# Joining an expert's two sorted slot lists by a reversed identity product instead of a second sort

## The chip, the cores and the metric

The kernel runs on one core of one Trainium2 chip. The metric is the device time of the whole program in microseconds (us), as a median of several runs. All engines of the core work at once, each through its own queue of instructions: TensorE (PE), VectorE (DVE), ScalarE (ACT), GpSimd (POOL) and SyncE (SP, which here only issues DMAs). They are held to one another by semaphores alone.

## What is computed

Two transformer layers, each a gated cross-attention and a gated feed-forward, over 2048 tokens of 256 numbers. The change lies in the feed-forward of the first layer, a mixture of 64 experts: each token chooses 8 experts, and each expert takes its tokens in token order up to a capacity of 128; what comes later is dropped.

```python
E, K = 64, 8
CAP = 128
def _moe_experts(x, topk_idx, topk_w, w_gate, w_up, w_down):
    flat_e = topk_idx.reshape(-1)
    rows = jnp.repeat(jnp.arange(n), K)
    oh = jax.nn.one_hot(flat_e, E, dtype=jnp.int32)
    pos = jnp.cumsum(oh, axis=0) - oh
    pos = jnp.take_along_axis(pos, flat_e[:, None], axis=1)[:, 0]
    valid = (pos < CAP).astype(x.dtype)
    p = jnp.minimum(pos, CAP - 1)
    buf = jnp.zeros((E, CAP, H), x.dtype).at[flat_e, p].add(x[rows] * valid[:, None])
    g = jnp.einsum('ech,ehi->eci', buf, w_gate)
    u = jnp.einsum('ech,ehi->eci', buf, w_up)
    y = jnp.einsum('eci,eih->ech', jax.nn.silu(g) * u, w_down)
    y_tok = y[flat_e, p] * (topk_w.reshape(-1) * valid)[:, None]
    return jnp.zeros((n, H), x.dtype).at[rows].add(y_tok)
```

The result is a sum over the slots of an expert, row by row; the order of the tokens within the 128 slots doesn't enter it, only which tokens are in.

## The kernel before

The program goes through four stages, one after the other: the attention of layer one (to about 400 us), its routing and experts (400 to 744 us), the attention of layer two, and its mixture of 8 experts. The tokens are worked in 4 groups of 512.

**Routing.** For each group of tokens the kernel computes scores and the 8 chosen experts of each token. To each pair of token and chosen expert it gives a key, larger the earlier the token comes, and zero where the expert isn't chosen. `keyT` holds the keys transposed: partition e is expert e with the tokens of the first half (0 to 1023), partition 64 + e is the same expert with the tokens of the second half, 1024 keys to a partition.

**Slot lists.** Inside the DVE program, `largest(dst, src)` finds the 128 largest keys of each partition in order, 8 at a time: 16 times a `max` (L901; the trace calls it MAX8), and between them 15 times a `match_replace` (L904), which strikes out the 8 just found. The trace shows each `match_replace` as two instructions, MATCH_VALUE_LOAD and MATCH_REPLACE8. Each instruction waits for the one before. `largest` runs twice: over `keyT` into `cand` (all 128 partitions, 1024 keys each), which leaves two sorted lists to an expert, one on partition e and one on 64 + e; then, after a DMA by SP has laid the second list beside the first (L407, `cand[0:64, 128:256]`), over these 256 candidates into `slots` (64 partitions). PE transposes `slots` (L1742), ACT copies the result out of PSUM into `slotsT` (L1370), slot by partition and expert by column. The rest of this part waits for it:

```python
dve.wait_ge(t_ring.free, T3)
sl.add(dve.tensor_scalar(part[0][:, 0:E0], slotsT[:], -1.0, float(K0 * T), ALU.mult, ALU.add))
sl.add(dve.tensor_scalar(part[1][:, 0:E0], slotsT[:], 0.0, None, ALU.is_equal))
...
sl.add(dve.tensor_tensor(dst_idx[:], src_idx[:], part[1][:, 0:E0], ALU.add))
```

`src_idx` is the row of the DRAM tensor `table` to gather for each slot (an empty slot has key 0 and takes the row of zeros, 2048). `dst_idx` is the row to add to; an empty slot gets 2048 + its own partition, so that the 128 rows of an expert are always different ones.

**Experts.** 32 steps of two experts. For each step POOL issues two indirect gathers of 128 rows (L479, `xg` from `table`), PE transposes the rows (L1750), multiplies (L1764, L1777), DVE scales into `y` (L947), and POOL issues two indirect DMAs that add the rows to two DRAM sums, `acc` (L489); each waits until the one before it on the same sum has landed. Gathers run three steps ahead. SP loads the weights of 8 experts ahead and then one step's for each step done.

**Rings.** PE writes PSUM banks in turn within a ring, here `t_ring` with two banks. Each fill has a fixed position; `full` counts fills, `free` counts reads. PE waits before a fill until the position two back has been read; a reader waits for its own position. T3 is the position of the first fill of the experts.

Of the kernel before, what the change touches and what calls it, by code (L numbers as in the profile page):

```python
# [8 lines left out]
ACT = mybir.ActivationFunctionType  # L9
ALU = mybir.AluOpType  # L10
AX = mybir.AxisListType

P = 128
# [5 lines left out]
NG = NT // G  # L19
C = DIM // P  # L20
H0, D0 = 16, 128
E0, I0, K0 = 64, 88, 8
CAP = 128
# [78 lines left out]
def flamingo(nc, a, out, stages=4):  # L102
    with ExitStack() as ctx:
        def sb(name, shape, dt=F32, scope=ctx):
            return scope.enter_context(nc.sbuf_tensor(name, shape, dt))

        def sem(name):
            return ctx.enter_context(nc.semaphore(name))
# [5 lines left out]
        t_ring = Ring([bank[4], bank[5]], sem("t_full"), sem("t_free"))  # L114
# [5 lines left out]
        ident = sb("ident", [P, P])  # L120
        ones = sb("ones", [P, P])
# [23 lines left out]
        before = sb("before", [P, 8, 8])  # L145
        key_base = sb("key_base", [P, NT])
        zeros = sb("zeros", [P, ROW])
        cand = sb("cand", [P, 2 * CAP])
        slots = sb("slots", [E0, CAP])
        slotsT = sb("slotsT", [P, E0])  # L150
        spare = sb("spare", [P, E0])
        src_idx = sb("src_idx", [P, E0], I32)
# [45 lines left out]
        keyT = sb("keyT", [P, T // 2], scope=rows)  # L198
# [102 lines left out]
        rows_ready = sem("rows_ready")  # L301
        slot_chain = sem("slot_chain")
        slots_ready = sem("slots_ready")
        cand_ready = sem("cand_ready")
        cand_moved = sem("cand_moved")
        idx_ready = sem("idx_ready")
        idx_now = sem("idx_now")
        w_loaded = [sem(f"w_loaded{q}") for q in range(4)]
# [32 lines left out]

        Q2, S2, T2 = Q_STEP * NG, S_PREP + S_STEP * NG, T_STEP * NG
        QR, SR, TR, TRF = 2, 2, 4, 3
        Q3, S3, T3 = Q2 + QR * NG, S2 + SR * NG, T2 + TR * NG + 1
        NQ = E0 // 8
        Q4, S4, T4 = Q3 + 4 * NQ, S3 + 4 * NQ, T3 + 4 * NQ
        QA, SA, TA = 4, 8, 18
# [8 lines left out]
        def _(sp):  # L356
# [46 lines left out]
                    SKV - MAIN)).then_inc(w3_loaded, 16)  # L403
            sp.dma_start(ctx_rows[:], ctx_d[0:P, :]).then_inc(ctx_loaded, 16)

            sp.wait_ge(cand_ready, 1)
            sp.dma_start(cand[0:E0, CAP:2 * CAP], cand[E0:P, 0:CAP]).then_inc(cand_moved, 16)  # L407
            with sp.Fori(1, NQ) as i:
                for q in range(4):

# [39 lines left out]
        def _(pool):  # L450
            pool.memset(ident[:], 0.0).then_inc(ident_zero, 1)
            pool.wait_ge(ident_zero, 1)
            pool.memset(zeros[:], 0.0).then_inc(zero_ready, 1)
            pool.memset(before[:], 1.0).then_inc(ident_zero, 1)
            pool.iota(key_base[:], pattern=[[-K0 * P * G, NG], [K0 - K0 * P, G]], base=K0 * T + 1,
                      channel_multiplier=-K0, allow_small_or_imprecise_dtypes=True).then_inc(r_const, 1)
# [4 lines left out]
                               base=0, pattern=[[1, 8], [-1, 8]], channel_multiplier=0).then_inc(r_const, 1)  # L461
            pool.affine_select(out=ident[:], in_=ident[:], compare_op=ALU.not_equal, fill=1.0,
                               base=0, pattern=[[-1, P]], channel_multiplier=1).then_inc(const_ready, 1)

            def split_squares(i):
                for h in range(H0):
                    pool.wait_ge(q2_ready, H0 * i + h + 1)
                    pool.tensor_tensor(q2_lo[:, h % 3, :], q2[h % 2], q2_hi[:, h % 3, :],  # L468
                                       ALU.subtract).then_inc(q2_split, 1)
# [53 lines left out]
            for n in range(NA):  # L523
# [4 lines left out]
                               pattern=[[-D1, 8]], channel_multiplier=1).then_inc(mask_step, 1)  # L528
            pool.wait_ge(mask_step, 2)
            pool.affine_select(out=head_mask[:], in_=head_mask[:], compare_op=ALU.is_ge, fill=0.0, base=D1 - 1,  # L530
                               pattern=[[D1, 8]], channel_multiplier=-1).then_inc(mask_step, 1)
# [8 lines left out]
        def _(dve):  # L540
# [357 lines left out]
            def largest(dst, src):  # L898

                for r in range(CAP // 8):  # L900
                    sl.add(dve.max(dst[:, 8 * r:8 * r + 8], src))  # L901
                    sl.wait()
                    if r < CAP // 8 - 1:
                        sl.add(dve.match_replace(src, dst[:, 8 * r:8 * r + 8], src, 0.0))  # L904
                        sl.wait()

            largest(cand[:, 0:CAP], keyT[:])
            dve.drain().then_inc(cand_ready, 1)
            dve.wait_ge(cand_moved, 16)
            largest(slots[:], cand[0:E0, :])  # L910
            dve.drain().then_inc(slots_ready, 1)

            dve.wait_ge(t_ring.free, T3)
            sl.add(dve.tensor_scalar(part[0][:, 0:E0], slotsT[:], -1.0, float(K0 * T), ALU.mult, ALU.add))
# [310 lines left out]
        def _(act):  # L1225
            sr, tr, qr = s_ring.end(), t_ring.end(), q_ring.end()
# [129 lines left out]
            def route(i, half, last):  # L1356
                tr.at(T2 + TRF, TR, i)
                if not last:
                    route_front(i + 1)
                rows = slice(half * E0, (half + 1) * E0)  # L1360
                act.activation(keyT[rows, bass.ds(G * P * (i - half * (NG // 2)), G * P)], tr.read(act)[rows, :],
                               ACT.Copy).then_inc(t_ring.free, 1)
# [3 lines left out]
            with act.Fori(NG // 2, NG - 1) as i:  # L1366
                route(i, 1, False)
            route(NG - 1, 1, True)
            tr.at(T2 + TR * NG)
            act.activation(slotsT[:], tr.read(act)[:, 0:E0], ACT.Copy).then_inc(t_ring.free, 1)  # L1370

            def transposed(q):
                act.activation(xgT[:, q % 2], tr.read(act)[:].rearrange(
# [171 lines left out]
        def _(pe):  # L1545
            qr, sr, tr = q_ring.end(), s_ring.end(), t_ring.end()
# [192 lines left out]
            route(NG - 1, True)  # L1739
            tr.at(T2 + TR * NG)  # L1740
            pe.wait_ge(slots_ready, 1)
            pe.transpose(tr.fill(pe)[:, 0:E0], slots[:], ident[0:E0, 0:E0]).then_inc(t_ring.full, 1)  # L1742

            def transpose_rows(i, q):
                pe.wait_ge(xg_loaded[q], 32 * (i + 1))
# [295 lines left out]
```

## Time and profile before

| | us |
|---|---|
| median of 3 runs | 1337.47 |
| lowest and highest | 1336.98, 1337.78 |
| the profiled execution's own time | 1336.93 |
| its span, first to last instruction | 1335.2 |
| of it, the first search over `keyT` | 469.75 to 509.73 |
| from there to the first use of `slotsT` | 509.73 to 527.29 |
| experts, first PE work to the last scatter landed | 534.13 to 744.20 |

The profile is of one execution; its time lies 0.54 us under the median. Its page has the span in 40 slices of some 33 us with the busy tenths of each engine, the chain of work that ended last, and groups of instructions by line. From its trace come timelines (start, duration, engine, line, what), groups by shape, the chain in order of time, and busy times by stretch. PEclk is TensorE's granted clock: 0.50 is 1.2 GHz and 1.00 is 2.4 GHz, a number between is a mean over a stretch.

### The profile page before, as it was taken

What the parts mean: (1) busy time and instruction counts of PE and PEld (TensorE: products, weight loads), DVE (VectorE), ACT (ScalarE), POOL (GpSimd) and SP (SyncE); (2) the same over time, 40 slices, a digit from 0 to 9 for tenths busy, and PEclk for the clock granted to TensorE, in tenths of its full rate; (3) what the DMA queues carried; (4) which work ended last, traced back from release to release, by engine and by line L of the source; (5) the groups of instructions that cost most, each with busy time, mean ns of one, the idle gap of its engine ahead of it and who ended that gap; (6) DMA issues with size and microseconds to landing.
All of it is one profiled execution on the core that took longest, in us unless ns stands there. A gap on an engine that the chain in (4) does not pass through costs nothing.

```text
span 1335.2 us, 16322 instructions
## 1 busy us (share of the span) xinstructions
PE 1038.4 (78%) x5301; PEld 855.8 (64%) x5301; DVE 697.9 (52%) x1659; ACT 431.5 (32%) x793; POOL 278.2 (21%) x223
## 2 busy tenths in 40 slices
PE   5989979989766400776667368887989999999997
PEld 3867858778545300665556226564657989898996
DVE  6277586675758897222223477575675324232221
ACT  4565465554623100111111032324252232322221
POOL 0414214133000001788787110010100000000000
PEclk8999999999887655888787566757666999899899
DMA  7004000000001040788786540000000000000001
GB/s 266 3 0 137 1 1 1 0 1 1 1 0 40 24 126 11 170 173 180 166 186 120 144 164 1 2 0 0 0 0 0 1 1 0 0 0 0 0 0 64
DMA packets 58967, 66.36 MB, mean 50 GB/s; under 512 B 5037, under 2 KB 55719, under 8 KB 58151
## 3 DMA queue, kind: packets, MB, share of 16 engines
q1 hardware_dynamic: 45268, 46.48, 11.1%
q0 software_dynamic: 12288, 18.88, 8.1%
q8 instruction: 28, 0.46, 0.1%
q10 hardware_dynamic: 1363, 0.37, 0.1%
q14 instruction: 20, 0.16, 0.0%
HBM read 48.13 MB, written 17.56 MB: 49 GB/s over the span
## 4 chain that ended last, share of the span: by engine, by line
PE 54%; DVE 14%; issue 12%; DMA 6%; ACT 6%; POOL 6%; ACTq 0%; DVEq 0%; POOLq 0%; SPq 0%
PE bank L1959 12%; PE bank L1978 7%; DMA acc<-y,dst_now 5%; PE bank L1619 4%; PE bank L1664 4%; PE bank L1887 3%; PE bank L1845 3%; PE bank L1649 3%; POOL acc L489 2%; PE bank L1970 2%; POOL xg L479 2%; PE bank L1904 2%; POOL q_lo L468 2%; DVE cand L901 1%; PE bank L1804 1%
## 5 line engine op out<-in xcount | busy, mean ns | idle before, releaser
L1959 PE MATMUL bank<-gu_hi,xnT_split 128*128 128x352 f32 x640 | 158.7, 328 | 0.0
L468 POOL TENSOR_TENSOR q_lo<-soft,q_hi 128x512 fp32r<-128x512 f32 x64 | 93.2, 1456 | 236.8 <-ACT soft L1313 236.7
L1959 PEld LDWEIGHTS bank<-gu_hi,xnT_split 128*128 128x128 f32 x640 | 112.6, 190 | 1.0 <-issue 0.7
L479 POOL DMA_INDIRECT xg<-table,src_now x64 | 63.9, 999 | 216.5 <-DVE src_now L927 197.4
L489 POOL DMA_INDIRECT acc<-y,dst_now x64 | 102.3, 1599 | 26.7 <-issue 20.3
L1959 PE MATMUL bank<-gu_lo,xnT_split 128*128 128x352 f32 x320 | 103.8, 324 | 0.0
L1183 DVE SCALAR_TENSOR_TENSOR soft<-sg,combine_w,bank 128x176 f32<-128x176 f32 x160 | 56.4, 395 | 87.4 <-PE bank L1959 81.3
L1978 PE MATMUL bank<-dn,attnT 128*128 128x256 f32 x448 | 101.2, 384 | 0.0
L1978 PEld LDWEIGHTS bank<-dn,attnT 128*128 128x128 f32 x448 | 85.6, 194 | 11.2
L707 DVE COPY qT<-bank 128x512 f32<-128x512 f32 x64 | 44.2, 691 | 87.7 <-PE bank L1664 86.6
L1517 ACT ACTIVATE sg<-bank 128x352 f32<-128x352 f32 x80 | 37.1, 464 | 152.0 <-PE bank L1959 151.9
L947 DVE TENSOR_SCALAR y<-bank,xg 128x256 f32<-128x256 f32 x64 | 28.0, 480 | 106.6 <-PE bank L1777 106.6
L627 DVE SCALAR_TENSOR_TENSOR x<-bank,gates,x 128x256 f32 (+1 forms) x48 | 22.7, 482 | 114.0 <-PE bank L1978 94.8
L1764 PEld LDWEIGHTS bank<-xgT,w_gu 128*88 128x88 f32 x512 | 75.8, 193 | 6.7 <-issue 3.8
L1764 PE MATMUL bank<-xgT,w_gu 128*88 128x128 f32 x512 | 77.3, 316 | 0.7 <-issue 0.7
L1750 PE MATMUL bank<-ident,xg 128*128 128x128 f32 x128 | 25.7, 335 | 65.5 <-DMA xg<-table,src_now 65.5
L1309 ACT ACTIVATE q_hi<-qT 128x512 fp32r<-128x512 f32 x64 | 40.4, 630 | 91.3 <-DVE qT L707 91.2
L1619 PE MATMUL bank<-vw,attnT 128*128 128x256 f32 x256 | 62.1, 399 | 4.3 <-ACT attnT L1263 4.3
L1649 PE MATMUL bank<-kT,qT 128*128 128x64 f32 x512 | 64.0, 268 | 0.0
L1649 PEld LDWEIGHTS bank<-kT,qT 128*128 128x128 f32 x512 | 62.5, 191 | 1.4
L1750 PEld LDWEIGHTS bank<-ident,xg 128*128 128x128 f32 x128 | 17.4, 169 | 70.1 <-DMA xg<-table,src_now 56.5
L1959 PEld LDWEIGHTS bank<-gu_lo,xnT_split 128*128 128x128 f32 x320 | 60.7, 190 | 0.3
(256 smaller groups left out, 2140.1 us busy)
## 6 DMA issues: line engine op xcount, KB each, us to landing
w_gu<-in_L_ffn_w_gu SPq DMA_DIRECT2D x32, 352.0 KB
w_dn<-in_L_ffn_w_down SPq DMA_DIRECT2D x32, 176.0 KB
acc<-zeros SPq DMA_DIRECT2D x2, 2176.0 KB, 11.4
acc_rows<-acc SPq DMA_DIRECT2D x8, 512.0 KB, 4.9
gu<-in_L_gu SPq DMA_DIRECT2D x1, 3520.0 KB, 13.7
table<-xw SPq DMA_DIRECT2D x4, 640.0 KB
wo<-in_L_xattn_Wo SPq DMA_DIRECT2D x2, 1024.0 KB, 16.2
wq<-in_L_xattn_Wq SPq DMA_DIRECT2D x1, 2048.0 KB, 18.5
```

The lines of the kernel that those rows point to most:

```text
L468: pool.tensor_tensor(q2_lo[:, h % 3, :], q2[h % 2], q2_hi[:, h % 3, :], ALU.subtract).then_inc(q2_split, 1)
L479: pool.indirect_dma_start(xg[:, q, e, :], None, table, bass.IndirectOffsetOnAxis(ap=src_now[:, q, e:e + 1], axis=0)).then_inc(xg_loaded[q] ...
L489: pool.indirect_dma_start(acc[e], bass.IndirectOffsetOnAxis(ap=dst_now[:, q, e:e + 1], axis=0), y[:, q, e, :], None, compute_op=ALU.add).t ...
L707: dve.tensor_copy(qT[:, h % 3, :], qr.read(dve)[:]).then_inc(q_ring.free, 1)
L1183: ins = dve.scalar_tensor_tensor(out=act_v[:, j % 2, at:at + F1], in0=sg[:, (j + p) % 2, e * F1:(e + 1) * F1], scalar=combine_w[:, j, 2 * ...
L1619: mm = pe.matmul(o_banks[0][:, 0:DIM], attnT[:, j % 2, p, :], vw[:, j // 2, p, :], start=(p == 0), stop=(p == 7))
L1649: mm = pe.matmul(s_bank[0][:, at:at + SKV], qT[:, h % 3, j * P:(j + 1) * P], kT[:, h, (j // 2) * SKV:(j // 2 + 1) * SKV], start=True, stop ...
L1664: mm = pe.matmul(b[:], w[:, c, h * D0:(h + 1) * D0], v[:, c, :], start=(n == 0), stop=(n == len(terms) - 1))
L1750: mm = pe.transpose(b[:, at:at + P], xg[:, q, e, c * P:(c + 1) * P], ident[:])
L1764: mm = pe.matmul(b[0:I0, e * P:(e + 1) * P], w_gu[:, q, e, c, o:o + I0], xgT[:, q % 2, e, c, :], start=(c == 0), stop=(c == C - 1))
L1959: mm = pe.matmul(b[:, 0:2 * F1], v[:, c, j * P:(j + 1) * P], w[:, c, p, o, :], start=(n == 0), stop=(n == len(terms) - 1))
L1978: mm = pe.matmul(o_banks[j % 2][:, 0:DIM], attn_flat[0:n, f, :], dn1[0:n, f, :], start=(f == 0), stop=(f == FC - 1))
```

## The change

The second `largest` and the DMA between the two are gone. `cand` has 128 columns now, `slots` is gone. In their place come four products on PE and five instructions on DVE. With a_e the count of expert e's first list:

- PE transposes `cand` whole: the columns 0 to 63 are the first lists, the columns 64 to 127 the second, slot by partition. DVE copies this into `lists`.
- DVE marks the used slots of the first lists (`taken`), PE multiplies by a matrix of ones, and so each partition has a_e for each column e.
- DVE forms `keep` = (a_e + own partition number < 128), and `late` = second list times `keep`: of the second list the first 128 - a_e entries.
- PE sums identity times first list and `reversal` times `late` in one PSUM bank. `reversal` has its ones where row + column is 127; so the second list lies from slot 127 downward and meets the first nowhere.
- DVE copies the sum into `slotsT`, which ACT did before.

`reversal` is built by POOL at the start of the program with a memset and an affine_select. The ring `t_ring` has three fills here, not one, so T3 is two higher. The slots of an expert hold the same tokens in another order: second-half tokens stand in falling order at the end, and empty slots in the middle.

```diff
-        cand = sb("cand", [P, 2 * CAP])
-        slots = sb("slots", [E0, CAP])
+        cand = sb("cand", [P, CAP])
+        lists = sb("lists", [P, 2 * E0])
+        taken = sb("taken", [P, E0])
+        keep = sb("keep", [P, E0])
+        late = sb("late", [P, E0])
+        reversal = sb("reversal", [P, P])
...
-        Q3, S3, T3 = Q2 + QR * NG, S2 + SR * NG, T2 + TR * NG + 1
+        Q3, S3, T3 = Q2 + QR * NG, S2 + SR * NG, T2 + TR * NG + 3
...
-            sp.wait_ge(cand_ready, 1)
-            sp.dma_start(cand[0:E0, CAP:2 * CAP], cand[E0:P, 0:CAP]).then_inc(cand_moved, 16)
...
+            pool.memset(reversal[:], 0.0).then_inc(reversal_ready, 1)
             pool.memset(before[:], 1.0).then_inc(ident_zero, 1)
...
+            pool.wait_ge(reversal_ready, 1)
+            pool.affine_select(out=reversal[:], in_=reversal[:], compare_op=ALU.not_equal, fill=1.0,
+                               base=1 - P, pattern=[[1, P]], channel_multiplier=1).then_inc(reversal_ready, 1)
...
-            largest(cand[:, 0:CAP], keyT[:])
-            dve.drain().then_inc(cand_ready, 1)
-            dve.wait_ge(cand_moved, 16)
-            largest(slots[:], cand[0:E0, :])
+            largest(cand[:], keyT[:])
             dve.drain().then_inc(slots_ready, 1)
+            lr = t_ring.end()
+            lr.at(T2 + TR * NG)
+            dve.tensor_copy(lists[:], lr.read(dve)[:, 0:2 * E0]).then_inc(t_ring.free, 1)
+            lr.evacuated(dve)
+            dve.tensor_scalar(taken[:], lists[:, 0:E0], 0.0, None, ALU.is_gt).then_inc(list_step, 1)
+            dve.tensor_scalar(keep[:], lr.read(dve)[:, 0:E0], spare[:, 0:1], float(CAP), ALU.add,
+                              ALU.is_lt).then_inc(t_ring.free, 1)
+            lr.evacuated(dve)
+            dve.tensor_tensor(late[:], lists[:, E0:2 * E0], keep[:], ALU.mult).then_inc(list_step, 1)
+            dve.tensor_copy(slotsT[:], lr.read(dve)[:, 0:E0]).then_inc(t_ring.free, 1)
...
-            tr.at(T2 + TR * NG)
-            act.activation(slotsT[:], tr.read(act)[:, 0:E0], ACT.Copy).then_inc(t_ring.free, 1)
...
-            pe.transpose(tr.fill(pe)[:, 0:E0], slots[:], ident[0:E0, 0:E0]).then_inc(t_ring.full, 1)
+            pe.transpose(tr.fill(pe)[:, 0:P], cand[:], ident[:]).then_inc(t_ring.full, 1)
+            pe.wait_ge(list_step, 1)
+            pe.matmul(tr.fill(pe)[:, 0:E0], ones[:], taken[:], start=True, stop=True).then_inc(t_ring.full, 1)
+            pe.wait_ge(list_step, 2)
+            pe.wait_ge(reversal_ready, 2)
+            b = tr.fill(pe)[:, 0:E0]
+            pe.matmul(b, ident[:], lists[:, 0:E0], start=True, stop=False)
+            pe.matmul(b, reversal[:], late[:], start=False, stop=True).then_inc(t_ring.full, 1)
```

On DVE, between the last `max` over `keyT` and the arithmetic on `slotsT`, the program of before reads as follows (its first rows; the pair L904, L901 stands 15 times in all):

```order
550 L901 MAX cand<-keyT 128x8
551 L904 MATCH_REPLACE keyT<-cand,keyT 128x1024
552 L901 MAX cand<-keyT 128x8
553 L901 MAX slots<-cand 64x8
554 L904 MATCH_REPLACE cand<-slots,cand 64x256
555 L901 MAX slots<-cand 64x8
```

And the changed one in the same place:

```order
551 L910 MATCH_REPLACE keyT<-cand,keyT 128x1024
552 L907 MAX cand<-keyT 128x8
553 L917 COPY lists<-bank 128x128
554 L919 TENSOR_SCALAR taken<-lists 128x64
555 L920 TENSOR_SCALAR keep<-bank,spare 128x64
556 L923 TENSOR_TENSOR late<-lists,keep 128x64
557 L924 COPY slotsT<-bank 128x64
558 L927 TENSOR_SCALAR soft<-slotsT 128x64
```

Of DVE's 31 instructions over 64 partitions none is left; five over 128 partitions stand there.

On PE, between the last transposes of the routing (of keys in `soft`) and the first of the experts (of `xg`), before:

```order
795 L1734 MATMUL bank<-ident,soft 128x128 x4
796 L1742 MATMUL bank<-ident,slots 128x64
797 L1750 MATMUL bank<-ident,xg 128x128 x4
```

and now:

```order
795 L1745 MATMUL bank<-ident,soft 128x128 x4
796 L1753 MATMUL bank<-ident,cand 128x128
797 L1755 MATMUL bank<-taken,ones 128x64
798 L1759 MATMUL bank<-lists,ident 128x64
799 L1760 MATMUL bank<-late,reversal 128x64
800 L1768 MATMUL bank<-ident,xg 128x128 x4
```

One transposition has become four products, the last two into one bank.

## Rows read from the trace of the kernel before

**Rows 1.** Page, section 2: busy tenths in 40 slices of 33 us, DVE, POOL, PEclk

```profile
DVE  6277586675758897222223477575675324232221
POOL 0414214133000001788787110010100000000000
PEclk8999999999887655888787566757666999899899
```

**Rows 2.** Busy time by stretch: window, length, busy us (instructions), clock, DMA share, GB/s

```profile
core 0: us, PE busy (x) PEld busy (x) DVE busy (x) ACT busy (x) POOL busy (x), PEclk, DMA share, GB/s
470.00:509.75 39.75, 0.00 (x0) 0.00 (x0) 38.68 (x46) 0.00 (x0) 0.00 (x0) 0.50 0.32 85
509.75:527.29 17.54, 0.37 (x1) 0.18 (x1) 13.89 (x46) 0.22 (x1) 0.00 (x0) 0.50 0.01 2
534.13:744.20 210.07, 137.85 (x769) 120.73 (x769) 52.69 (x168) 31.23 (x64) 162.73 (x125) 0.80 0.77 161
```

**Rows 3.** Chain that ended last, in order of time: start, us, what

```profile
508.49 1.24 DVE cand L901
...
509.81 1.78 DMA cand<-cand
...
511.61 0.43 DVE slots L901
512.04 0.02 issue
512.06 0.49 DVE cand L904 x2
...
526.11 0.43 DVE slots L901
526.54 0.03 issue
...
526.63 0.38 PE bank L1742
527.01 0.02 issue
527.04 0.23 ACT slotsT L1370
527.27 0.02 issue
527.29 0.20 DVE soft L914
```

**Rows 4.** Prices of nearby operations: engine, line, shape, count, busy us, mean ns, idle before

```profile
L1742 PE MATMUL bank<-ident,slots 64*128 64x64 f32 x1 | 0.4, 367 | 57.5 <-DVEq L911 57.5
L1046 DVE COPY c<-bank 128x256 f32<-128x256 f32 x16 | 6.8, 423 | 14.3 <-PE bank L1887 14.3
L726 DVE TENSOR_SCALAR qvar<-bank 128x64 f32<-128x64 f32 x4 | 0.9, 214 | 0.0
L918 DVE TENSOR_TENSOR soft<-soft,spare 128x64 f32<-128x64 f32 x1 | 0.2, 217 | 0.0
L914 DVE TENSOR_SCALAR soft<-slotsT 128x64 f32<-128x64 f32 x1 | 0.2, 196 | 0.8 <-ACT slotsT L1370 0.8
```

**Rows 5.** Timeline, first expert step: start, duration, engine, line, what, idle before

```profile
529.72 1.15 POOL L479 DMA_INDIRECT xg<-table,src_now  x1 [197.36 <-DVE src_now L927]
534.13 1.11 PE L1750 MATMUL bank<-ident,xg 128*128 128x128 f32 x4 [7.13 <-DMA xg<-table,src_now]
535.28 0.60 ACT L1373 ACTIVATE xgT<-bank 128x512 f32<-128x512 f32 x1 [8.02 <-PE bank L1750]
535.98 3.54 PE L1764 MATMUL bank<-xgT,w_gu 128*88 128x128 f32 x16 [0.73 <-issue]
539.63 0.42 DVE L939 TENSOR_TENSOR act_h<-act_g,bank 88x256 f32<-88x256 f32 x1 [10.78 <-PE bank L1764]
540.11 1.13 PE L1777 MATMUL bank<-w_dn,act_h 88*128 88x256 f32 x4
541.43 0.42 SPq L383 DMA_DIRECT2D w_gu<-in_L_ffn_w_gu  x1
```

**Rows 6.** Timeline, first scatters of two steps in mid-stage and one later; same columns

```profile
588.65 1.62 POOL L489 DMA_INDIRECT acc<-y,dst_now  x1 [0.30 <-issue]
...
595.08 1.62 POOL L489 DMA_INDIRECT acc<-y,dst_now  x1 [0.30 <-issue]
...
724.54 1.62 POOL L489 DMA_INDIRECT acc<-y,dst_now  x1 [0.30 <-issue]
```

**Rows 7.** The chain's shares from 527 to 744 us; then `acc`'s landings

```profile
by line: issue 30.6%; DMA acc<-y,dst_now 30.4%; POOL acc L489 13.4%; POOL xg L479 11.4%; DMA xg<-table,src_now 6.0%; PE bank L1777 2.1%; PE bank L1764 1.6%; PE bank L1750 1.5%; DVE y L947 0.9%; POOLq L487 0.3%; DVE act_h L939 0.2%; DVE src_
DMA to landing us min/median/max: 3.8/4.4/14.6
```

**Rows 8.** Timeline, first 7 us of the program

```profile
0.81 0.20 POOL L451 MEMSET ident<- 128x128 f32 x1 [0.29 <-POOLq L2012]
2.08 0.28 POOL L462 TENSOR_SCALAR_AFFINE_SELECT ident<-ident 128x128 f32<-128x128 f32 x1
6.72 0.29 PEld L1551 LDWEIGHTS bank<-ident,ctx_rows 128*128 128x128 f32 x2 [6.72 <-issue]
```

**Rows 9.** Timeline of ACT, attention of layer two: the table load in each loop body

```profile
793.24 1.28 ACT L1397 ACT_TABLE_LOAD   x1
856.16 1.28 ACT L1397 ACT_TABLE_LOAD   x1
917.73 1.28 ACT L1397 ACT_TABLE_LOAD   x1
```

More of the change, by code:

```diff
@@ L303, in flamingo @@
         slots_ready = sem("slots_ready")
-        cand_ready = sem("cand_ready")
-        cand_moved = sem("cand_moved")
+        reversal_ready = sem("reversal_ready")
+        list_step = sem("list_step")
         idx_ready = sem("idx_ready")
```

## The prediction, made before the changed kernel ran

> **What bounds the kernel now.** I read the slices of the page first, for the place of the change. In slices 15 and 16 (some 467 to 534 us) DVE stands at 9 and 7 tenths while POOL is at 0 and 1, and the granted clock is at 5, its low level [rows 1]. Busy time by stretch says it more sharply: from 470 to 509.75 us and again to 527.29 us DVE is the only engine at work, PE runs one product, DMA has a share of 0.01 in the second stretch [rows 2]. Nothing runs beside the search that could take its place on the path, and nothing that is under way could hold the next stage back.
>
> Then the chain of waits, for the edges [rows 3]. The last `max` over `keyT` ends at 509.73. From there the chain goes through the DMA that moves the second lists, through 16 `max` and 15 `match_replace` on `slots`, one transposition on PE and one copy on ACT, and comes to the first arithmetic on `slotsT` at 527.29. This stretch of 17.56 us is what the change rewrites, and all of it lies on the path.
>
> Last, what follows. The first gather is issued at 529.72, after an idle time of POOL of 197 us that DVE's indices ended, and PE's first expert work waits for that gather's landing [rows 5]. Then POOL and the landings of the scatters set the pace: POOL is busy for 163 of 210 us [rows 2], of the chain 30.4% is landing of `acc` and 25% POOL's own issue of gathers and scatters [rows 7], and one step takes 595.08 - 588.65 = 6.43 us [rows 6]; from 588.65 to 724.54 are 21 steps, 6.47 us each, so the rhythm is even. SP's first further weight load, at 541.43, is let go by the first step's output, not by the clock on the wall [rows 5]. So the whole stage can start earlier as a block, and with it all that is behind.
>
> **What goes.** The DMA with its hops: 511.61 - 509.73 = 1.88 us. The second search: 16 x 0.43 (`max`) + 15 x 0.49 (`match_replace` with its load) + 30 gaps of some 0.02 = 14.93 us, the 526.54 - 511.61 of the chain. Transposition and copy with their hops: 527.29 - 526.54 = 0.75 us. Together 17.56 us [rows 3].
>
> **What comes**, step by step, on the same path, since each step needs the one before. The granted clock is 0.50 in this stretch, 1.2 GHz, after 40 us in which PE did nothing [rows 2], and a handful of small products gives me no reason to price them at the other level.
>
> 1. DVE's last `max` to PE: 0.09 us, as 526.54 to 526.63 [rows 3].
> 2. Transposition with 128 columns. That with 64 took 0.37 [rows 4]. A further 64 columns: 16 products of 128 columns took 3.54 us in the first expert step, 0.22 each, so 0.11 for 64 [rows 5]. 0.48.
> 3. Hop of 0.03 and DVE's copy of 128 columns from PSUM. The rows have 0.214 for 64 columns and 0.423 for 256 [rows 4]; on the line between, 0.28 to 0.29. Together 0.32.
> 4. `taken`: 0.20 as L914, and a gap of 0.02 [rows 3, 4]: 0.22.
> 5. Hop from DVE to PE 0.05 (540.05 to 540.11 [rows 5]), the product with ones 0.37, hop back 0.03: 0.45.
> 6. `keep` from PSUM 0.21 and `late` 0.22 with a gap of 0.02 between: 0.45 [rows 4].
> 7. Hop 0.05, first product 0.37, the second behind it 0.11, hop 0.03: 0.56.
> 8. Copy into `slotsT` 0.21, gap 0.02: 0.23.
>
> The sum is 0.09 + 0.48 + 0.32 + 0.22 + 0.45 + 0.45 + 0.56 + 0.23 = 2.80 us. The gain is 17.56 - 2.80 = 14.76 us.
>
> Bounds. Two terms are not shown by any row as they will stand: a product right behind another of 64 columns with other weights, and the hops into a PE that waits for two semaphores. If the second product costs its full 0.37 and each of the three later hops 0.09 more (one more hop of the kind of step 1), the new chain takes 2.80 + 0.26 + 0.27 = 3.3, and with 0.3 more for what I overlook, 3.6. If the hops are all 0.02 and the copies no dearer than 0.21, it takes 2.5. So the gain lies between 13.9 and 15.1 us; I stay at 14.76, since the nearest rows are of just this kind of chain.
>
> The rows price a product by its columns: 0.22 us for 128 columns at the low clock [rows 5]. The Trainium skill ("FP8 and Floating Point Precision", TensorE Precision Notes) has true FP32 take four passes through the array, which would be 4 x 128 / 1.2 GHz = 0.43 us for 128 columns, as an estimate. The row holds about half of that. By the page's price the 64 further columns of step 2 and the second product of step 7 would cost 0.21 each, the new chain 3.0 us and the gain 14.6.
>
> **What is moved or added elsewhere.** POOL builds `reversal`: a memset ahead of the work on `ident`, 0.20 us, and an affine_select behind it, 0.28 [rows 8]. So `ident` is ready at 2.56, not 2.36, and PE first wants it at 6.72, when the data has landed: hidden, with 4.2 us to spare. If that cover were gone it would cost 0.2 us. ACT loses one copy; its next instruction waits for PE at 535.28 anyway [rows 5]. SP loses a wait and a DMA; behind them stood only weight loads that are held by the experts' first output. The ring gives no new wait: the third fill needs the first one read (step 3, long done), and the experts' first fill needs the second one read (step 6); the bank is the same one as before, since T3 rises by two.
>
> The arithmetic behind `slotsT`, the four index copies, the 0.85 us to POOL's first gather and the landing of that gather are untouched and move as they are. What is late next is this gather, as now; nothing else is near, as the first stretch's DMAs (share 0.32) have given way to 0.01 after 509.75 [rows 2].
>
> The sum against the profiled execution: 1336.93 - 14.76 = 1322.2. The median of the runs lies 0.54 above that execution, so I forecast 1322.7 us.
>
> **Rivals.**
>
> *A, the clock falls otherwise.* The attention of layer two runs at mean clocks of 0.5 to 0.7 [rows 1], so PE is there often at the low level, and a shift of all by 14.8 us could make other stretches slow or fast. The price is in the table loads, which mark the same place of one loop body: 856.16 - 793.24 = 62.92 and 917.73 - 856.16 = 61.57 us [rows 9]. Two passes over the same code differ by 1.35 us; over four groups that is at most 5.4 if all fall on one side, more likely 1 to 3. Time: 1317 to 1328. For it: the clock there is really unsettled. Against it: three runs of before lie within 0.80 us, so that what differs from run to run doesn't reach the total. The level follows from what PE did before, and that sequence stays the same once the block has moved. The Trainium skill ("TensorE: Matmul & The Clock Gate", What's actually happening) adds that the moment at which the clock is let up is not tied to the kernel's start and varies from run to run; by that rule a shift of the block is one more draw of what the three runs drew already, which speaks for small.
>
> *B, the order of rows makes the scatters slower, and the kernel ends slower than before.* The slots hold the same rows in another order: the second list falls, and empty slots, which all gather row 2048, stand in the middle. If the DMAs of an expert landed later for it, the steps would stretch, since 30.4% of 217 us, 66 us, are landings of `acc` on the chain [rows 7]. To eat up 14.8 us and 2.7 more for a result called slower, these 66 us must grow by 17.5, or 27%: a median landing of 5.6 instead of 4.4 us. At that point it decides; 10% (4.8 us) would give back 6.6 us and end at 1329. Against it: the number and size of rows are unchanged, rows of an expert are scattered over the table anyway, and 21 steps with experts of whatever load went by at an even 6.47 us [rows 6].
>
> *C, the change doesn't free the path.* Something other than the slots would hold the first gather: a table write, the zeroing of the sums, weights. Then it would end at 1337.5 minus little. The DMA share of 0.01 in the stretch and POOL's wait that DVE ended [rows 2, 5] speak against it.
>
> **How the numbers follow.** Forecast as summed (gain of 13.9 to 15.1 with a scatter of 1 us more either way): 0.82. A with more than 2 us in either direction: 0.11. B giving back a part: 0.03; B to a slower kernel: 0.02. C: 0.02. The range takes the bounds of the unknown terms (1322.4 to 1323.6), the typical 1 to 3 us of A on both sides, and nothing of B beyond that: 1319.5 to 1326.5 us. What lies outside is the rest of A (0.03), B and C. About 0.2%, 2.7 us, is what a measurement of this kernel can tell from no change. Faster by more than that: 0.82 + 0.11 + 0.03 = 0.96, of which I leave 0.01 for the edge of B: 0.95. Within it: C and that edge, 0.03. Slower: 0.02.
>
> **What would show it.** In the profile after: no DMA from `cand`, a stretch of 2.5 to 3.6 us from the last `max` to the first arithmetic on `slotsT`, at a granted clock of 0.50; the first gather near 515.0 instead of 529.72; steps of 6.43 to 6.47 us; the last scatter landed near 729.4 instead of 744.20; passes of 60 to 63 us in the attention of layer two. I am wrong if the new stretch is above 4 us (then a hop or a product is mis-sized), if the expert steps are longer (B), or if the two later stages together differ from 591.0 us (1335.2 - 744.2) by more than 3 (A).

## The result and the profile after

| | us |
|---|---|
| changed kernel, median of 4 runs (lowest, highest) | 1320.73 (1319.32, 1321.93) |
| kernel before, median of 4 runs beside it | 1337.22 (1334.33, 1337.78) |
| ratio, 95% interval | 0.9884 (0.9870 to 0.9899) |
| profiled execution of the changed kernel, its span | 1319.32, 1317.6 |

Faster by 16.5 us, with an interval of 13.5 to 17.4 us; the forecast was 1322.7 us in 1319.5 to 1326.5, a gain of 14.8. In two later series of runs the same kernel took 1321.60 us (6 runs, ratio 0.9895, 0.9874 to 0.9917) and 1320.77 us (5 runs, 0.9888, 0.9867 to 0.9909). Over all series the kernel before has 39 runs with a mean of 1336.60 us and the changed one 15 with 1321.51: a difference of 15.1 us.

The place of the change, in the timeline of the profiled execution: start, duration, engine, line, operation, and in brackets the idle time before it and what ended that. It answers to [rows 3].

```profile
508.18 1.23 DVE L907 MAX8 cand<-keyT 128x8 f32<-128x1024 f32 x1
509.52 0.47 PE L1753 MATMUL bank<-ident,cand 128*128 128x128 f32 x1 [40.75 <-DVEq L914]
510.03 0.29 DVE L917 COPY lists<-bank 128x128 f32<-128x128 f32 x1 [0.62 <-PE bank L1753]
510.36 0.20 DVE L919 TENSOR_SCALAR taken<-lists 128x64 f32<-128x64 f32 x1
510.61 0.69 PE L1755 MATMUL bank<-taken,ones 128*128 128x64 f32 x2 [0.61 <-DVE taken L919]
511.33 0.28 DVE L920 TENSOR_SCALAR keep<-bank,spare 128x64 f32<-128x64 f32 x1 [0.78 <-PE bank L1755]
511.65 0.22 DVE L923 TENSOR_TENSOR late<-lists,keep 128x64 f32<-128x64 f32 x1
511.93 0.69 PE L1759 MATMUL bank<-lists,ident 128*128 128x64 f32 x2 [0.63 <-DVE late L923]
512.41 0.64 PE L1760 MATMUL bank<-late,reversal 128*128 128x64 f32 x2
513.09 0.23 DVE L924 COPY slotsT<-bank 128x64 f32<-128x64 f32 x1 [1.21 <-PE bank L1760]
513.34 0.20 DVE L927 TENSOR_SCALAR soft<-slotsT 128x64 f32<-128x64 f32 x1
...
515.77 1.15 POOL L485 DMA_INDIRECT xg<-table,src_now  x1 [183.67 <-DVE src_now L940]
```

I call the stretch from the end of the last MAX8 (508.18 + 1.24 = 509.42) to the first use of `slotsT` (513.34) the join. It is 3.92 us, where it was 17.56: the join itself gave 13.64 us. The first gather follows 2.43 us behind, as it did behind 527.29 [rows 3, 5]. What to see on PE's lines is the count: the transposition is one instruction (x1), each of the three other products is two (x2).

The same by stretch: length, busy us and count of each engine, granted clock, DMA share, GB/s. The first two answer to the second and third line of [rows 2]; the last two are loop passes in the attention of layer two, each from one of ACT's table loads, shown below, to the next.

```profile
core 0: us, PE busy (x) PEld busy (x) DVE busy (x) ACT busy (x) POOL busy (x), PEclk, DMA share, GB/s
509.42:513.34 3.92, 2.28 (x7) 1.61 (x7) 1.22 (x5) 0.00 (x0) 0.00 (x0) 0.50 0.00 0
520.19:729.92 209.73, 138.89 (x769) 121.47 (x769) 53.59 (x168) 31.28 (x64) 162.88 (x125) 0.80 0.77 161
...
777.60:838.10 60.50, 50.85 (x187) 34.63 (x187) 42.34 (x97) 21.19 (x37) 4.05 (x4) 0.72 0.01 2
838.10:899.52 61.42, 50.65 (x187) 35.18 (x187) 38.33 (x90) 21.21 (x37) 4.05 (x4) 0.72 0.00 1
```

```profile
777.60 1.28 ACT L1408 ACT_TABLE_LOAD   x1
838.10 1.28 ACT L1408 ACT_TABLE_LOAD   x1
899.52 1.28 ACT L1408 ACT_TABLE_LOAD   x1
```

In the kernel before, the same two passes, from 793.24 and from 856.16 [rows 9], were

```profile
793.24:856.16 62.92, 52.94 (x187) 37.01 (x187) 40.97 (x94) 21.20 (x36) 4.04 (x4) 0.67 0.01 2
856.16:917.73 61.57, 52.81 (x187) 36.79 (x187) 38.36 (x90) 21.21 (x37) 4.04 (x4) 0.67 0.00 1
```

PE has the same 187 products in each, busy for 52.9 us at a clock of 0.67 and for 50.7 at 0.72. So of the 17.6 us between the two profiled spans, 13.64 are the join; 0.31 lie ahead of it (509.73 against 509.42, where only POOL's two instructions at the start of the program are new); 0.35 in the experts, from the first gather to POOL's first instruction after the last scatter (214.53 against 214.18); and 3.3 in the two later stages (590.95 against 587.65), which the change doesn't touch. Of these 3.3 us, 2.42 lie in the first of the two passes and 0.15 in the second; the part ahead of them is 1.34 us shorter (47.65 against 48.99), and what follows them is 0.61 us longer (418.08 against 417.47). In the second pass PE is busy for 2.2 us less and the pass is only 0.15 us shorter, so the mean clock alone doesn't set the length of a pass. The experiments ask what these 3.3 us are, why the join took 3.92 and not 2.80 us, and whether it can be shorter.

### The profile page after: what moved, and what is told of

The parts are those of the page before. It is cut to its first block and busy times, and to the rows that moved or that the text cites. A ratio compares the mean times of both kernels' runs of the same rounds, so it can differ in the third digit from the quotient of the medians.

```text
span 1317.6 us, 16309 instructions
## 1 busy us (share of the span) xinstructions
PE 1034.8 (79%) x5307; PEld 852.9 (65%) x5307; DVE 686.0 (52%) x1618; ACT 431.5 (33%) x792; POOL 278.8 (21%) x225
## 3 DMA queue, kind: packets, MB, share of 16 engines
HBM read 48.13 MB, written 17.56 MB: 50 GB/s over the span
## 5 line engine op out<-in xcount | busy, mean ns | idle before, releaser
L1782 PEld LDWEIGHTS bank<-xgT,w_gu 128*88 128x88 f32 x512 | 79.5, 202 | 7.6 <-issue 5.6
L1782 PE MATMUL bank<-xgT,w_gu 128*88 128x128 f32 x512 | 82.9, 331 | 0.7 <-issue 0.7
L1384 ACT ACTIVATE xgT<-bank 128x512 f32<-128x512 f32 x32 | 19.1, 597 | 152.5 <-PE bank L1768 152.5
```

The source lines that it names most:

```text
L1782: mm = pe.matmul(b[0:I0, e * P:(e + 1) * P], w_gu[:, q, e, c, o:o + I0], xgT[:, q % 2, e, c, :], start=(c == 0), stop=(c == C - 1))
```

## Experiments

The surplus is what the total gained beyond the join's 13.64 us. Three theories of it: the later stages draw anew from some sequences of clock levels in each run (1, scatter); the new place in time fixes another sequence (2, place); something in the kernel is faster for good (3).

**The changed kernel again**, without an edit, for more runs.

> The changed kernel once more, for the size of its gain with more runs. Its first profile had 13.6 us from the join itself, 0.3 from the stages ahead of it, 0.3 from the experts and 3.3 from the attention of layer two (17.6 in all). Theory 1 (the 3.3 us are scatter of the clock, a draw that falls anew in each run): the difference of medians comes down towards 13.6 to 14.5 us, and runs of one kernel differ by up to 3 us. Theory 2 (the new position in time sets another sequence of clock levels for good) and theory 3 (something else in the kernel, such as the order of rows or the addresses, is faster for good): the difference stays at 16 to 17 us.

1321.60 us (1319.30 to 1324.70, 6 runs), the kernel before 1336.42 (1333.37 to 1339.79, 15 runs), a difference of medians of 14.8 us, between what theory 1 (13.6 to 14.5) and the other two (16 to 17) had forecast. Join 3.93 us. Here the search ended at 510.76, 1.3 us later than in the first profile, and the two passes took 62.79 and 60.32 us. So one and the same program has other passes from one execution to the next (60.50 and 61.42 us in the first profile), and the runs of one kernel spread over 5.4 and 6.4 us. Both speak for theory 1, but the changed kernel's own median stayed within 1 us of the first.

**Pads behind the join**: 11, 6 and later 2 dependent passes of DVE over `keyT`, which nobody reads any more.

```diff
             dve.tensor_copy(slotsT[:], lr.read(dve)[:, 0:E0]).then_inc(t_ring.free, 1)
+            for _ in range(6):
+                sl.add(dve.tensor_scalar(keyT[:], keyT[:], 1.0, None, ALU.mult))
+                sl.wait()
```

> The changed kernel with 11 dependent passes of DVE over 128x1024 numbers behind the join, some 11 x 1.25 = 13.7 us, so that the experts start where they did before the change. Theory 1: the time of the changed kernel plus the length of the pad, some 1334.5 us, and within 1 us of the kernel before if that draws the same lot. Theory 2: exactly the time of the kernel before, and the clock levels of its attention of layer two (0.67 in the loop passes) come back. Theory 3: some 2 to 3 us under the kernel before, though all starts at the same moment.

> The same with 6 passes, some 7.5 us. Theories 1 and 3: the changed kernel plus 7.5 us within 1 us. Theory 2: off this line by 1 to 3 us in either direction, since a third position draws a third sequence of clock levels.

A pass took 0.72 us, not 1.25: DVE's line of the 11 passes and the one of the 6, in the two timelines,

```profile
514.93 7.97 DVE L927 TENSOR_SCALAR keyT<-keyT 128x1024 f32<-128x1024 f32 x11
```

```profile
514.39 4.33 DVE L927 TENSOR_SCALAR keyT<-keyT 128x1024 f32<-128x1024 f32 x6
```

So the pads were 7.9 and 4.3 us, and the first didn't put the block back where it was; it started its gathers 4.4 us earlier than the kernel before (525.36 against 529.72). My estimate had taken MATCH_REPLACE8's 1.21 us for 1024 columns as the price of any pass. The times are 1331.79 (10 runs) and 1327.67 us (6 runs), 10.6 and 6.5 us above 1321.2, the middle of the changed kernel's two medians so far, for pads of 7.9 and 4.3: both slower by 2.2 to 2.7 us than the pad. Taken by the expectation, with 4.3 in place of 7.5 us, the run with 6 passes misses theories 1 and 3 (within 1 us) and falls where theory 2 had put it (off by 1 to 3 us). Against theory 2 stands the profile with 6 passes. Its experts end 9.4 us earlier than those of the kernel before (734.81 against 744.25), and yet the two passes have the kernel before's length to 0.01 us, at its clock:

```profile
783.80:846.72 62.92, 52.94 (x187) 37.01 (x187) 40.96 (x94) 21.21 (x36) 4.04 (x4) 0.67 0.01 1
846.72:908.29 61.57, 52.81 (x187) 36.78 (x187) 38.37 (x90) 21.22 (x37) 4.04 (x4) 0.67 0.00 1
```

The same two passes, begun at another moment: a pass falls into a small set of lengths (over all profiles 60.3 to 60.5, 61.4 to 61.6 and 62.7 to 62.9 us), and being later or earlier doesn't by itself choose. That the clock makes the difference is argued, not shown: the passes of 60.3 to 60.5 us all have a mean clock of 0.72 and those of 62.7 to 62.9 us have 0.67 or 0.70, but those of 61.4 to 61.6 us occur at 0.67, 0.69, 0.70 and 0.72.

**The join by a maximum.** The first list is zero just in the slots where the second belongs, and each key of the second half is smaller than each of the first. So neither a count nor a mask is needed. ACT copies the transposed first list out, while DVE reverses the second.

```diff
-            dve.tensor_copy(lists[:], lr.read(dve)[:, 0:2 * E0]).then_inc(t_ring.free, 1)
...
-            dve.tensor_copy(slotsT[:], lr.read(dve)[:, 0:E0]).then_inc(t_ring.free, 1)
+            dve.tensor_copy(rev[E0:P, :], cand[E0:P, ::-1]).then_inc(list_step, 1)
+            lr.skip(1)
+            b = lr.read(dve)
+            dve.wait_ge(t_ring.free, T3 - 1)
+            dve.tensor_tensor(slotsT[:], b[:, 0:E0], lists[:, 0:E0], ALU.max).then_inc(t_ring.free, 1)
...
+            act.activation(lists[:, 0:E0], tr.read(act)[:, 0:E0], ACT.Copy).then_inc(t_ring.free, 1)
...
+            pe.transpose(tr.fill(pe)[:, 0:E0], cand[0:E0, :], ident[0:E0, 0:E0]).then_inc(t_ring.full, 1)
+            pe.wait_ge(list_step, 1)
+            pe.transpose(tr.fill(pe)[:, 0:E0], rev[E0:P, :], ident[E0:P, E0:P]).then_inc(t_ring.full, 1)
```

> The join in another way: keys of the first half are all larger than keys of the second, and the first list is zero where the second belongs, so slotsT is the maximum of the first list and the second one read backwards. DVE copies the second lists backwards while PE transposes the first and ACT copies them out; PE transposes the second, DVE takes the maximum. No product with ones, none with reversal. From the last max over keyT to the first arithmetic on slotsT: copy 0.3, hop 0.05, transposition 0.45, maximum 0.25, hops 0.1, some 1.2 us against 3.92. All theories: 2.7 us under the changed kernel, some 1318 us; if only the full fp32 products are dear, as the trace of the changed kernel says, the four transpositions and copies cost no more than that.

The join is as expected (1.09 against some 1.2 us). Timeline, same columns:

```profile
510.84 1.23 DVE L908 MAX8 cand<-keyT 128x8 f32<-128x1024 f32 x1
512.18 0.36 PE L1754 MATMUL bank<-ident,cand 64*128 64x64 f32 x1 [40.75 <-DVEq L915]
512.21 0.22 DVE L918 COPY rev<-cand 64x128 f32<-64x128 f32 x1
512.49 0.36 PE L1756 MATMUL bank<-ident,rev 64*128 64x64 f32 x1
512.58 0.22 ACT L1382 ACTIVATE lists<-bank 128x64 f32<-128x64 f32 x1 [40.52 <-PE bank L1754]
512.91 0.22 DVE L922 TENSOR_TENSOR slotsT<-bank,lists 128x64 f32<-128x64 f32 x1 [0.48 <-PE bank L1756]
513.17 0.20 DVE L925 TENSOR_SCALAR soft<-slotsT 128x64 f32<-128x64 f32 x1
```

From 512.08 to 513.17 it is 1.09 us, 2.83 less than in the changed kernel. Each PE line is x1, each some 0.36 us. The time was 1321.41 us (6 runs), only 0.2 us under the changed kernel in the same series and 3.4 above the 1318 that I had expected. In this profile the search ends at 512.08, 1.3 us later than in the changed kernel's second profile, and the experts take 215.24 instead of 212.74 us. Since neither stage was edited, I ran it again.

> The join by the maximum once more, since its join took 1.09 us as expected (2.83 under the changed kernel) but its median of 6 runs lay only 0.2 us under it. If that was scatter (its profiled execution had the search end 2.7 us later than that of the changed kernel, ahead of the join): 1318 to 1320 us, 16.5 to 18 us under the kernel before in the same call. If something in this form costs the 2.6 us back for good: 1321 to 1322 us, and the same stage longer again in the profile.

1318.29 us (1317.71 to 1321.74, 5 runs), 17.45 us under the kernel before beside it (ratio 0.9870, 0.9849 to 0.9891); join again 1.09 us. The two medians of the same program disagree by 3.1 us, more than the 2.8 us in question. The mean of the 11 runs is 1320.61 us, against 1321.51 for the 15 of the changed kernel: the total doesn't settle which is faster. That the join itself is shorter by 2.83 us is shown in both profiles.

**The counting product in fp32r**, one execution. fp32r is a 32-bit type for operands of PE; the counted numbers are 0 and 1, which it holds exactly.

```diff
-        taken = sb("taken", [P, E0])
+        taken = sb("taken", [P, E0], F32R)
+        ones_r = sb("ones_r", [P, P], F32R)
...
+            dve.tensor_copy(ones_r[:], ones[:]).then_inc(list_step, 1)
             largest(cand[:], keyT[:])
...
-            pe.matmul(tr.fill(pe)[:, 0:E0], ones[:], taken[:], start=True, stop=True).then_inc(t_ring.full, 1)
+            pe.matmul(tr.fill(pe)[:, 0:E0], ones_r[:], taken[:], start=True, stop=True).then_inc(t_ring.full, 1)
```

> The changed kernel with the ones and the marks taken rounded to fp32r for the counting product (both hold only 0 and 1, so the sums stay exact). In the changed kernel this product shows as two pairs of weight load and MATMUL, 0.69 us for 64 columns. If a full fp32 product is dear because it goes through the array as two instructions: one pair here, some 0.35 us, and the join 3.92 - 0.34 = 3.6 us. If it is dear for another reason (the wait, the weights of ones): 0.69 us as before.

Timeline:

```profile
513.55 0.42 PE L1757 MATMUL bank<-taken,ones_r 128*128 128x64 f32 x1 [0.61 <-DVE taken L921]
...
514.61 0.69 PE L1761 MATMUL bank<-lists,ident 128*128 128x64 f32 x2 [0.64 <-DVE late L925]
```

One instruction and 0.42 us, where the full fp32 product beside it still has two and 0.69. The join is 3.66 us, 0.26 shorter. So what is dear is the second instruction of a full fp32 product, not the wait ahead of it, which is the same (0.61 us idle in both kernels). The whole run took 1326.05 us, 4.5 above the changed kernel's mean. Its search ended at 512.36, ahead of the join and up to 2.9 us later than in other profiles, and the two later stages took 592.17 us. What follows the two passes took 422.10 us here, 422.03 in the second profile of the kernel before and 420.64 in the run with PE kept busy, against 417.35 to 418.50 in the ten other profiles. Since the unedited kernel before does it too, I take this for scatter and not for the edit; why it differs is open.

**PE kept busy ahead of the join**, one execution (1326.68 us).

```diff
+            pe.wait_ge(o_read, 2 + 2 * NT)
+            pe.wait_ge(slot_chain, 26)
+            for n in range(10):
+                pe.matmul(o_banks[0][:, 0:ROW], ones[:], zeros[:], start=True, stop=True)
             pe.wait_ge(slots_ready, 1)
```

> The changed kernel with 10 extra products of ones and zeros on PE, 320 columns each, beside the last three rounds of the search (PE waits for the 13th match_replace), so that PE isn't idle ahead of the join. If the granted clock of 0.50 is what makes the join's products long: clock above 0.5 in the join, the transposition 0.47 down to some 0.3, the three later products together 1.8 down to some 1.2, join 3.0 to 3.3 us instead of 3.92. If the hops and fixed times do: 3.7 or more. The other stages as in the changed kernel.

The ten products took 8.04 us, longer than the 6.3 us that the search still had, so the first transposition came late, and the join, counted from the end of the search, was 4.49 us. From that transposition on it can be read:

```profile
503.77 8.04 PE L1755 MATMUL bank<-zeros,ones 128*128 128x320 f32 x20 [34.36 <-DVE keyT L910]
...
511.64 0.27 PE L1757 MATMUL bank<-ident,cand 128*128 128x128 f32 x1
...
512.53 0.43 PE L1759 MATMUL bank<-taken,ones 128*128 128x64 f32 x2 [0.61 <-DVE taken L919]
```

```profile
511.64:514.55 2.91, 1.37 (x8) 0.82 (x6) 1.22 (x5) 0.00 (x0) 0.00 (x0) 1.00 0.00 0
```

At a granted clock of 1.00 instead of 0.50 the same steps take 2.91 us, where the changed kernel took 513.34 - 509.52 = 3.82: transposition 0.27 instead of 0.47, counting product 0.43 instead of 0.69. So 0.9 us of the join is the low clock. The whole join comes out at 2.91 + 0.10 = 3.0 us by this, the lower end of what was expected. Of the 2.91 that remain PE is busy for 1.37; the other 1.54 are hops and DVE's instructions.

**Both: the maximum, and six such products**, short enough to end before the search.

> The join by the maximum, with 6 extra products on PE beside the last three rounds of the search, short enough to end before it. Each transposition at the fast clock some 0.2 us shorter (0.27 instead of 0.47 in the run with 10 such products), the second one alone on the path: join 0.85 to 1.0 us instead of 1.09. In the total not to be told from the join by the maximum without them: 1318 to 1322 us.

```profile
511.45:512.45 1.00, 0.55 (x2) 0.28 (x2) 0.45 (x2) 0.22 (x1) 0.00 (x0) 1.00 0.00 0
```

Join 1.00 us, at a clock of 1.00, as expected; 1320.38 us (1317.11 to 1322.19, 5 runs), ratio to the kernel before 0.9875 (0.9854 to 0.9897). Of the two transpositions only the second one is on the path, and its 0.09 us is all that the clock gives here.

**The kernel before, a second profile (one execution, 1337.84 us); the changed kernel a third time; a pad of two passes.**

> The kernel before once more, for a second profile of its stages. If the stages scatter by themselves: the end of the search within 509.4 to 512.1 us, the loop passes in the attention of layer two between 60.3 and 62.9 us, join again 17.56 us to 0.02.

> The changed kernel once more. Time less the length of the join gives the rest of the program: so far 1317.6 us for the changed kernel (mean of 10 runs), 1318.9 for the kernel before (28), 1320.0 and 1319.4 with pads of 7.9 and 4.3 us, 1319.5 for the join by the maximum (11). If this is scatter: the rest comes out here nearer 1319, the time nearer 1322.5 to 1323. If the changed kernel's place in time is luckier for good: again 1317 to 1318, the time 1321 to 1322.

> The changed kernel with two passes behind the join, 1.45 us by the length of the pads so far (0.72 us a pass). Scatter: the rest of the program 1318 to 1320, the time 1323.5 to 1325.5. Place: nothing can be said in advance but that it would repeat to 0.5 us.

The changed kernel: 1320.77 us (1319.83 to 1324.09, 5 runs). By the expectation that speaks for a lucky place (1321 to 1322 us; time less join, the rest, 1317 to 1318) and against scatter (1322.5 to 1323). With two passes: 1323.94 us (1323.07 to 1325.88, 6 runs), which is the one for scatter (1323.5 to 1325.5). All the profiles by stage, in us; the end of the search is where the first stages end, the experts are from the first gather to POOL's first instruction after the last scatter, and "later" is the rest of the span:

| kernel | end of search | join | experts | passes in attention | later | span |
|---|---|---|---|---|---|---|
| before | 509.73 | 17.56 | 214.53 | 62.92, 61.57 | 590.95 | 1335.2 |
| before, 2nd | 510.73 | 17.56 | 213.06 | 62.72, 60.26 | 592.33 | 1336.1 |
| changed | 509.42 | 3.92 | 214.18 | 60.50, 61.42 | 587.65 | 1317.6 |
| changed, 2nd | 510.76 | 3.93 | 212.74 | 62.79, 60.32 | 588.94 | 1318.8 |
| changed, 3rd | 510.63 | 3.92 | 213.68 | 60.37, 61.41 | 588.34 | 1319.0 |
| pad of 2 | 510.63 | 5.25 | 213.97 | 62.71, 61.61 | 590.02 | 1322.3 |
| pad of 6 | 510.58 | 8.17 | 213.63 | 62.92, 61.57 | 590.89 | 1325.7 |
| pad of 11 | 511.12 | 11.81 | 214.34 | 62.88, 61.54 | 590.20 | 1329.9 |
| count in fp32r | 512.36 | 3.66 | 213.68 | 60.28, 61.41 | 592.17 | 1324.3 |
| PE kept busy | 510.06 | 4.49 | 214.99 | 62.79, 61.56 | 592.93 | 1324.9 |
| maximum | 512.08 | 1.09 | 215.24 | 62.72, 61.59 | 589.87 | 1320.7 |
| maximum, 2nd | 511.65 | 1.09 | 214.76 | 62.72, 61.61 | 590.07 | 1320.0 |
| maximum, PE busy | 511.45 | 1.00 | 212.98 | 60.26, 62.72 | 588.74 | 1316.6 |

Only the join answers to the edits, to 0.01 us where it repeats. All other columns move by 2.5 to 5.3 us from profile to profile, in stages that are the same instructions. That such scatter exists is so shown; that it is a draw of clock levels, as theory 1 has it, is not. But take the mean time of each kernel less its join, which is the rest of the program:

| kernel | runs | mean time | rest | standard error |
|---|---|---|---|---|
| before | 39 | 1336.60 | 1319.0 | 0.35 |
| changed | 15 | 1321.51 | 1317.6 | 0.45 |
| pad of 2 | 6 | 1324.32 | 1319.1 | 0.44 |
| pad of 6 | 6 | 1327.56 | 1319.4 | 0.62 |
| pad of 11 | 10 | 1331.81 | 1320.0 | 0.53 |
| maximum | 11 | 1320.61 | 1319.5 | 0.57 |
| maximum, PE busy | 5 | 1319.75 | 1318.8 | 0.90 |

Six of seven agree on 1318.8 to 1320.0. The changed kernel lies 1.45 us under the kernel before, with an error of 0.57, and it lay under it in each of the three series (by 2.3, 0.8 and 1.5 us); in its three profiles the two later stages took 587.65 to 588.94 us, in the ten others 588.74 to 592.93. One value of seven at 2.5 standard errors may be chance. It may also be that the exact place of the changed kernel's block draws the better sequences more often. A property of the changed code (theory 3) is the least likely, since the pads keep all of it and lose the surplus. Theory 2 and chance are not told apart by these runs. This stays open: 1.45 us, a tenth of the gain.

## Why the prediction was right, and where it was wrong

**What bounds and what goes: right.** The join lay wholly on the path, and all that is behind it started 13.95 us earlier, at the first gather. The 17.56 us that go are confirmed by the second profile of before to 0.01 us. (The terms that I gave for the second search add up to 14.83 us, not 14.93; the total goes by the chain and isn't touched.)

**What comes: 3.92 us against a sum of 2.80 and an upper bound of 3.6, so that the join's gain of 13.64 us lies below the 13.9 to 15.1 that I gave.** By the terms of the sum, from the timeline above:

| step | forecast | measured |
|---|---|---|
| 1, hop to PE | 0.09 | 0.10 |
| 2 and 3, transposition, hop, copy | 0.80 | 0.84 |
| 4, `taken` | 0.22 | 0.20 |
| 5, hop, counting product, hop | 0.45 | 0.77 |
| 6, `keep` and `late` | 0.45 | 0.54 |
| 7, hop, two products, hop | 0.56 | 1.22 |
| 8, copy | 0.23 | 0.25 |

The mis-sized terms are steps 5 and 7, by 0.32 and 0.66 us. I took 0.37 us for a product of 64 columns from L1742, which is a transposition, and 0.11 for 64 further columns from L1764, whose 16 lines I read as 16 products of 128 columns. They are 8 products of two instructions each: the trace counts instructions, and the program has 8 there per step. A full fp32 product shows twice in the trace, a transposition once. So a product of 128 columns costs 2 x 0.22 = 0.44 us there (at a mean granted clock of 0.54, not at 0.50 throughout as I wrote), and the run with fp32r shows it from the other side (one instruction, 0.42 instead of 0.69 us). The Trainium skill ("FP8 and Floating Point Precision", TensorE Precision Notes) has four passes for true FP32, 0.43 us by my estimate in the prediction. The trace agrees with that time, 0.44 us, once the lines are paired rightly, though it shows two instructions and not four; my sentence that the row holds half of it was wrong. `keep` cost 0.28, not 0.21: the TENSOR_SCALAR on `qvar` that I took for it [rows 4] has no scalar that is read per partition, as `keep` has. A second pair of rows differs likewise: the scaling into `y`, with such a scalar, takes 0.48 us for 128x256 out of PSUM and a copy of that size 0.42. That this is the reason I haven't tested.

**The clock of the new stretch: right.** Granted clock 0.50, and the run with PE kept busy shows what it costs, 0.9 us of 3.92.

**What is moved elsewhere: right.** `ident` was ready at 2.51 us (its affine_select started at 2.23 and took 0.28), and PE's first product waits for the context rows until 6.70 us; no new wait on the ring, on ACT or on SP shows.

**Rival A: the mechanism is there, the size of the scatter I had wrong.** I let three runs within 0.80 us stand for the scatter of the total. 39 runs of the kernel before lie between 1332.83 and 1340.21 us with a standard deviation of 2.1 us. The scatter isn't in the clock of the attention of layer two alone: the end of the search moves by 2.9 us over the profiles and the experts by 2.5. In the first comparison the scatter fell to the good side (13.64 us from the join, 16.5 in the medians), and that hid the 1.1 us by which the join was dearer than my sum. With that alone the forecast would have been 1323.8 us, still within the range; that the measured time came out below the forecast and not above it is luck. The loop passes were to last 60 to 63 us, which held; the later stages differ from 591.0 by 3.35 us in the first profile, just over the limit of 3 that I had set as a sign for A, so by my own sign A came true there, inside the range that I gave it. My reason against A, that the sequence of levels stays the same once the block has moved, doesn't hold: the changed kernel's own passes differ from profile to profile.

**Rival B: fell.** With the slots in the new order the experts took 212.74 to 215.24 us in eleven profiles (mean 214.0), with the old order 213.06 and 214.53 (mean 213.8). The sign that I had named, longer steps, isn't there, and the median landing of `acc` is 4.4 us in the first profiles of both kernels (3.9 to 5.2 over all profiles, with experts of 214.8 and 215.2 us at these two ends); a difference of some tenths would be lost in this. **Rival C: fell**, POOL's first gather followed DVE's indices at once, at 515.77, and its release is named in the line above.

## What to carry to other kernels

Where two sorted lists of bounded length are joined, ask what order the consumer needs: here none, so a reversed copy and a maximum do in 1.1 us what a second search did in 17.6 and the reversal by products in 3.9; in the total of this kernel the last 2.8 us can't be told from scatter. Price a product in fp32 by a row of a product in fp32, not by a transposition, and pair the lines of the trace with those of the program before you divide a duration by a count. And take the scatter of a total from tens of runs, not from three; the stretch that the edit reaches repeats to 0.01 us in the profile where the total moves by 5.

## What the runs showed of the hardware that I had not expected

- A full fp32 product is two pairs of weight load and MATMUL in the trace: 0.69 us for 64 columns at the clock of 0.50, 0.43 at 1.00. In fp32r it is one pair, 0.42 us at 0.50. A transposition of fp32 is one pair, 0.36 us for 64 x 128 and 0.47 for 128 x 128 at 0.50, 0.27 at 1.00.
- Products of zeros with ones raise the granted clock: after 12 MATMULs of 320 columns in 6.10 us, or 20 in 8.04 us, PE stood at 1.00 in the join, and at 0.50 without them.
- DVE's TENSOR_SCALAR over 128x1024 fp32 in SBUF takes 0.72 us a pass, MAX8 1.23 and MATCH_REPLACE8 1.21. The Trainium skill ("VectorE: DVE Perf Modes", Mode 2×_2P) gives operations with one tensor operand in SBUF twice the rate even in fp32; the trace agrees, since TENSOR_TENSOR over 128x1024, with two tensor operands, takes 1.22 to 1.27 us (L650, L664 of the kernel before), and I should have sized the pads by it.
- DVE copies a row backwards (64x128, step -1) in 0.22 us; no forward copy of this shape stands in these traces to compare it with.
- A pass of the same loop over the same 187 products takes 60.3 to 60.5, 61.4 to 61.6 or 62.7 to 62.9 us, at mean clocks of 0.67 to 0.72; a pass of 61.4 to 61.6 us occurs at both ends of these clocks, and the same pair of passes came back to 0.01 us with the block 9.4 us earlier.
